# A routed eight-expert layer: tile experts read eight at a time, TensorE's first read put in front of tile 0, and one weighting moved on ScalarE

## The reference, cut to what matters

```
ys  = cond * 256**-0.5
d   = rsqrt((ys*ys) @ (W*W) + 1e-8)
y   = ((x * ys[:, None, :]) @ W) * d[:, None, :]
lang   = softmax(y @ lang_w.T + lang_b)                  # 4 languages
logits = y @ router_w.T + router_b + 0.1 * (lang padded, neighbours summed)
top_p, top_i = top_k(softmax(logits), 2);  top_p /= top_p.sum()
h   = gelu(y @ w1[e] + b1[e])                            # 256 -> 1024, exact gelu
out = h @ w2[e] + b2[e]                                  # 1024 -> 256
return x + sum over the two picked e of top_p * out
```

## Time and profile before

| | |
|---|---|
| median of 3 runs | 298.55 us (296.48 to 300.69) |
| profiled execution | 297.96 us, of which the span from first to last instruction is 296.2 us |
| TensorE busy (PE) | 272.3 us, 92% |
| ScalarE / VectorE / GpSimd busy | 195.7 / 189.2 / 179.4 us |
| mean granted TensorE clock | 0.976 |
| read from HBM, written | 27.61 MB, 9.64 MB |

### The profile page before, as it was taken

One profiled execution on the slowest core, in us unless ns is written; L12 is line 12 of the kernel. 1 busy time (PEld: TensorE's weight loads), 2 busy tenths in 40 slices (PEclk: granted clock), 3 DMA queues, 4 the chain that ended last, 5 costly groups with the idle time before them and its releaser, 6 DMA issues.

```text
span 296.2 us, 8964 instructions
## 1 busy us (share of the span) xinstructions
PE 272.3 (92%) x3066; PEld 223.1 (75%) x3066; DVE 189.2 (64%) x427; ACT 195.7 (66%) x426; POOL 179.4 (61%) x161
## 2 busy tenths in 40 slices
PE   8999988689999999999999999999999999999800
PEld 6878967588889998777777777777787878778400
DVE  1857788799699788565565565555655656556410
ACT  3356469599697898757767677677676676775500
POOL 8200056884666598676878577777767776464230
PEclk9999999979999999999999999999999999999975
DMA  6899996399874333465574644853544434323130
GB/s 145 325 400 388 353 348 206 109 314 460 306 191 90 56 57 72 56 101 65 76 91 77 87 70 78 76 91 64 83 77 74 75 74 76 51 39 38 20 35 0
DMA packets 39497, 39.93 MB, mean 135 GB/s; under 512 B 19504, under 2 KB 35328, under 8 KB 39296
## 3 DMA queue, kind: packets, MB, share of 16 engines
q1 hardware_dynamic: 31872, 28.89, 32.8%
q0 software_dynamic: 7552, 10.45, 23.0%
q10 hardware_dynamic: 32, 0.01, 0.0%
HBM read 27.61 MB, written 9.64 MB: 126 GB/s over the span
## 4 chain that ended last, share of the span: by engine, by line
PE 82%; DMA 5%; DVE 4%; issue 3%; ACT 2%; POOL 1%; POOLq 0%; DVEq 0%
PE ps L643 33%; PE ps L660 30%; PE ps L539 5%; PE ps L652 4%; PE ps L557 4%; DMA rows<-y_rows,idx 3%; DMA out<-onehot,idx 3%; PE ps L481 1%; PE ps L620 1%; DVE wsp L951 1%; PE ps L512 1%; PE ps L521 1%; ACT wsp L781 1%; PE ps L497 1%; POOL out L470 1%
## 5 line engine op out<-in xcount | busy, mean ns | idle before, releaser
L643 PEld LDWEIGHTS ps<-onehot,wsp 128*128 (+1 forms) x1872 | 130.7, 99 | 34.4 <-issue 1.1
L643 PE MATMUL ps<-onehot,wsp 128*128 128x128 f16 x1872 | 154.2, 220 | 0.8 <-ACT onehot L811 0.6
L827 ACT ACTIVATE pay<-ps,cur 128x128 f32<-128x128 f32 x312 | 117.4, 459 | 51.7 <-issue 37.9
L660 PE MATMUL ps<-wsp,pay 128*128 (+1 forms) x616 | 138.1, 316 | 1.2 <-DVE pay L1113 1.2
L470 POOL DMA_INDIRECT out<-onehot,idx x39 | 67.8, 1739 | 33.7 <-DMA out<-onehot,idx 15.3
L1113 DVE SCALAR_TENSOR_TENSOR pay<-pay,cur 128x512 f16<-128x512 f32 x72 | 54.9, 762 | 29.2 <-ACT pay L815 27.9
L439 POOL DMA_INDIRECT rows<-y_rows,idx x39 | 57.0, 1463 | 17.9 <-issue 11.0
L461 POOL TENSOR_SCALAR onehot<-onehot,cur 128x256 f32<-128x256 f32 x36 | 38.1, 1059 | 24.0 <-DVE onehot L1131 15.8
L660 PEld LDWEIGHTS ps<-wsp,pay 128*128 128x128 f16 x616 | 45.7, 97 | 6.9 <-issue 1.7
L1107 DVE TENSOR_SCALAR pay<-pay,cur 128x512 f16<-128x512 f32 x36 | 18.8, 521 | 26.0 <-ACT pay L827 26.0
L815 ACT ACTIVATE pay<-pay,cur 128x512 f16<-128x512 f32 x36 | 26.0, 722 | 1.2
(11 more groups left out here) (176 smaller groups left out, 195.5 us busy)
## 6 DMA issues: line engine op xcount, KB each, us to landing
stage<-in_L_ffn_w SPq DMA_DIRECT2D x9, 1024.0 KB, 10.6
wsp<-in_L_ffn_w SPq DMA_DIRECT2D x7, 1024.0 KB, 12.0
y_rows<-pay SPq DMA_DIRECT2D x4, 512.0 KB, 9.3
wsp<-in_x SPq DMA_DIRECT2D x3, 512.0 KB, 7.9
b2bc<-in_L_ffn_b SPq DMA_DIRECT2D x1, 1024.0 KB, 4.8
rows<-y_rows,idx POOLq DMA_INDIRECT x39
out<-onehot,idx POOLq DMA_INDIRECT x39, 4.1
wsp<-in_x SPq DMA_DIRECT2D x2, 256.0 KB, 5.5
```

The costliest lines, as they stand in the source:

```text
L643: last = mm(ps[:, HB + (2 * j + g) % RING, c * P:(c + 1) * P], wsp[:, bass.ds(e, 1), o:o + P].rearrange("p a f -> p (a f)"), xsp[:, j % RI ...
L660: last = mm(ps[:, OB + j % 2, 0:width], hsp[:, (2 * j + g) % NH, part, c, :], wsp[:, bass.ds(e, 1), o + w:o + w + width].rearrange("p a f ...
L827: last = a.activation(to, ps[:, HB + (2 * j + g) % RING, c * P:(c + 1) * P], ACT.Gelu, bias=cur[:, j % CURS, cc:cc + 1], scale=cur[:, j % ...
```

## The change

Three edits. BATCH goes from 31 to 8, so that each of the two engines reads `te` in four reads of 8, 8, 8 and 7 numbers (tiles 8, 16, 24, 32), each where the first tile of its batch is first asked for; on TensorE that is, from tile 16 on, in the middle of its list, behind the waits of the block with up(j, half 0) and in front of its first matmul. TensorE's first read, with its wait, moves from behind `sum_squares(3)` to in front of `transpose_rows(0)`. And on ScalarE `weigh(NT - 3)` moves from between the halves of the last tile to in front of `gelus(38, 0)`, behind `gelus(37, 1)`.

```diff
-BATCH = 31
+BATCH = 8
@@ TensorE
+            pe.wait_ge(te_ready, 1)
+            expert(E)
             transpose_rows(0)
             blocks((0, 0), None)
             transpose_rows(1)
             blocks((0, 1), None)
             sum_squares(3)
-            pe.wait_ge(te_ready, 1)
-            expert(E)
             for j in range(NT):
@@ ScalarE
             for j in range(NT):
-                if j == NT - 1:
-                    weigh(NT - 3)
                 gelus(j, 1)
                 if j + 2 < XACT:
                     copy_x(j + 2)
                 for n in HIGHS.get(2 * j + 1, ()):
                     split_high(n)
+                if j == NT - 2:
+                    weigh(NT - 3)
                 if j + 1 < NT:
                     gelus(j + 1, 0)
```

## The result

The changed kernel took 295.63 us in the median of 20 runs (294.85 to 298.01); the kernel before, beside it, 298.50 (296.07 to 300.69). The ratio is 0.9924 [0.9895, 0.9952], by which the change saves 2.3 us (2.9 by the medians). The profiled execution of after is one of its slowest, 298.01 us.

What follows compares the result with a forecast made beforehand. TensorE was taken to bound the kernel from about 60 to 272 us. On 297.96 us, -0.8 - 1.3 - 0.3 + 3.3 - 1.4 = -0.5 gave 297.5, set at 297.8 towards the median 298.55; range 294.8 to 301.5.

Steps and rivals of the forecast that it cites:

- First read moved, −0.8: At tile 2's transposes: TensorE's first read, moved before tile 0, costs nothing there and ends a wait, gaining 0.8 us.
- Clock behind it, −1.3: Behind tile 2's transposes, about 60 us: less idle time keeps TensorE's clock from falling, gaining 1.3 us.
- The first rival: At 60 us: the clock falls all the same, 1.3 us less gain, 298.8 us; chance 0.22.
- VectorE's shorter first read, −0.3: At tile 8, about 108 us: VectorE's read of 8 ends sooner, its part of h comes earlier, gaining 0.3 us.
- Three late reads, +3.3: TensorE at tiles 16, 24, 32: the array stands still 1.1 us at each read, costing 3.3 us (2.0 to 8.25).
- The size of a read: TensorE's read of 8 numbers: 0.55 us fixed plus 0.58 by the number, 1.15 us.
- The rival "all words": TensorE's late reads: time goes by the number alone, 0.72 us each, three stalls of 0.67, 296.2 us; chance 0.14.
- hardly 0.05 us of a read is covered: At TensorE's late reads: the sequencer is only 0.3 us ahead of the array, so queued matmuls hide almost nothing.
- The rival of hidden reads: TensorE's late reads: matmuls already queued cover them, three stalls of 0, 294.2 us; chance 0.06.
- The long read that takes the clock: TensorE's late reads: from about 1.7 us each, the idle time also halves the clock, 304.2 to 307.5 us; chance 0.08.
- VectorE's late reads, 0: VectorE's reads at tiles 16, 24, 32: hidden between parts of h in the wait for ScalarE, cost 0.
- The tail, −1.4: Last scatters: tile 36's no longer waits for ScalarE's weighting and follows the landing of the one before, gaining 1.4 us.

Runs made afterwards that it cites:

- the two comparisons: The changed kernel against the kernel before, measured twice with no edit between: 295.63 against 298.50 us, then 297.15 against 297.68 us.
- the pair with one read: Changed kernel with one TensorE read of 31 before tile 0, weighting at its old place or moved: 294.69 and 293.94 us, before 298.89.

## Why the prediction came out as it did

The forecast was 297.8 in a range of 294.8 to 301.5; measured were 295.63 and 297.15. The direction was right and small, as said, but the number owes something to luck: two terms of the sum had the wrong size, a cost 0.7 us too high and a gain 0.9 too low, and a third, a gain of 1.3, was not the change's own and nearly made up for both.

- *First read moved, −0.8*: −0.73 after, −0.75 where it alone was moved. Right, with its mechanism: the read of 2.80 us in front of tile 0 costs nothing either. Shown. The size holds where tile 2's rows land last. In four of the ten profiles with the new place (the second one of the changed kernel, both of the kernel with one read, and the one with other offsets) they had landed before, and to block (5, 0) it is 33.4 us, 1.4 less than the 34.74 of the old place without a fall.
- *Clock behind it, −1.3*: −1.6 between the two profiles, so the size of a fall was right (with the first term 2.3 together, against the 2.1 that I let pass VectorE). **The step from the read to the fall failed** (with the read gone the idle time shrinks, and the fall may go with it): the fall isn't bound to the read. The same idle time of 1.76 us in the same place had no fall behind it with only the weighting moved, nor had 1.77 us with VectorE's reads alone; filling it gave no time; and of the fourteen profiles six have a fall that begins at 48 to 52 us; in three of these the read stands at its old place, so behind the fall. What decides where it falls stays open. Moving the read does go with a higher mean clock: 0.980 or more in 21 of 66 executions with the read moved and in 1 of 100 with it at its old place. But this is no gain in time that can be seen: the three fastest executions of the changed kernel (294.85 to 295.06) had 0.973 to 0.978, the highest clocks (0.985 and 0.986) in the same comparison took 295.52 to 296.29, and the mean clock leaves out a part of the half-rate start. The difference of 2 us between the two comparisons is no larger than what the start alone does to an execution; how many runs of each had the late start was not recorded. The first rival, at 0.22 the second likeliest, had the price right (this term is none of the change's own gain), but not the place: none of the ten profiles with the read moved has a fall at 60 us.
- *VectorE's shorter first read, −0.3*: **this step failed.** Alone it gave −1.4. Two things in it were wrong. The first is the wait: I let VectorE's copy wait for GpSimd's weighting, until 111.31, and so gave VectorE 0.35 us; that wait did not exist, and VectorE gained 1.3. The second is what TensorE makes of it. I had measured that by how late the array was at 116.8, and there it is small in the trace of after as well (0.3 us, counted from block (7, 1)). But it was TensorE's *sequencer* that waited at the block's head for VectorE's part of h, 1.2 us later than need be. In before it came out of that with 0.2 us of lead; from then on it, not the array, set the pace, 2.71 us for a block on average up to block (15, 1), while the array needs 2.64 where its sequencer has lead: the gain on before grows from 0.28 us at block (9, 1) to 1.15 at block (15, 1), some 0.07 us a block. The 1.2 us come back as lead, which the array eats. The earlier trace rows showed this lead of 0.3 in the kernel before, and I used it for the reads' price only.
- *Three late reads, +3.3*: 2.5 measured, both as shift of the blocks and by taking them out. The size of a read was the step that failed: 1.15 us assumed for 8 numbers, the chip shows 0.60, outside the bounds of 0.8 to 1.6 that I had set for being right. The rival "all words" (0.72) was nearer, with 2.0 for the three; it missed that the read of 7 costs 1.07, and that the shift is a little more than the read's own length (0.70 for 0.60). The estimate from the Trainium skill, DMA: Bandwidth & Descriptors, section "Latency and other measured facts", 1.17, failed by more: its floor of about 600 ns is twice what a read of one number takes here (0.31); what it adds, that the compiler unrolls by four, fits the fours in these rows. The step "hardly 0.05 us of a read is covered" was right for the sequencer and wrong for the array: 0.26, 0.39 and 0.81 us of idle, since the lead that VectorE's edit had built (1.2 us) paid for the rest. The three stalls therefore don't show as 2.5 in the waits, and a reader of the waits alone would have said 1.5.
- *The rival of hidden reads* (a queue that holds work for the array) is refuted: each read delays the blocks by its whole length (0.63, 0.71 and 1.13 us for reads of 0.60, 0.60 and 1.07).
- *The long read that takes the clock*: refuted for these reads, as the longest idle was 0.81 us. Where reads are longer it comes true in part: 2.06 us of idle had no fall behind it, and 2.4 us had one that cost 1.8 us at once, near the 1.7 of the rival, and 1.0 by the end.
- *VectorE's late reads, 0*: no new wait of TensorE for VectorE in the middle tiles; right.
- *The tail, −1.4*: −1.46 between these profiles, 1.1 in the mean of all (4.1 us without the move, 3.0 with it). The mechanism is right, and the size is near the best case: the scatters land a little irregularly and then the move shows less (3.41 and 3.37 us instead of 2.85). By the medians of runs it could not be resolved (+0.13% by itself, 0.3 us in the pair with one read).

The account of the two profiles, at the last scatter: +2.47 from the start and −1.61 from the clock (neither the change's), −0.73, then from block (5, 0) to the last matmul −1.15 for the lead and +2.59 for the reads, and −1.46 in the tail: +0.11 (285.66 to 285.55). The change's own terms are −0.7 us in this pair; where tile 2's rows land early they are 0.7 better. The first comparison gave −2.3 by its ratio, the second −0.2, and 1.7 by the means of both. My sum had −1.3 for the clock, reads priced 0.7 us too high and VectorE's gain 0.9 too low; by itself each of these errors is larger than the −0.5 that came out. To this I had added half of the distance to the median.

The better kernel follows from the same terms: without its late reads on TensorE the change is worth −0.7 to −1.4, −1.1 and −1.1, so 2.9 to 3.6 us, and 1.6 more against an execution of before with the fall at 60 us. Its two sets of 6 runs gave 4.5 and 5.0 us by the medians, which is more than the terms give without that fall; runs of 6 leave about 1.3 us open either way.

## What to carry to other kernels

Where one engine sets the pace, look at two clocks of it, the array's and the sequencer's: a wait that cost the array 0.3 us here cost its sequencer 1.2, and in these blocks, whose matmuls carry registers, the lead was not rebuilt at the full clock (it stayed at 0.3 us). Put a read of registers where the engine waits anyway and read everything there; splitting a read pays only on the engine where the first number is what the others wait for. Batches of registers were cheapest here with a start and a length divisible by four. And before two profiles are compared, check whether both reached the first point behind the start at the same time; here executions of one program lay 2 to 3 us apart there.

## What the runs showed of the hardware

- A `TENSOR_LOAD` of int32 numbers from one partition into registers goes in fours where its start is divisible by 4: 1 number 0.31 us, 4 0.35, 8 0.60, 7 1.07, 31 2.80 on TensorE; from other starts each number costs about 0.26 to 0.33 (7 in 1.99, 10 in 2.62). On VectorE 8 take 0.60, 7 1.05, 31 3.06. An engine's first read is about 0.2 us longer (8 numbers 0.78 and 0.83). What in the program makes the fours was not looked into.
- TensorE's sequencer and array run nearly even on the blocks: 2.71 against 2.64 us for 32 matmuls with their register addresses; by an estimate from these, 1 us of the sequencer's lead lasts some 14 blocks.
- TensorE starts at half rate, until about 11 to 13 us in nine profiles and until 17 to 19 us in five, and this parts executions by 2 to 3 us at tile 0. The row of the granted clock can say 1.00 there: eight matmuls of L539 took 3.25 us in one such stretch and 2.04 at the full rate.
- The granted clock falls to 0.50 for some 3.4 us, but whether and where (near the start, at 48 to 52 us, at 60 us) differs between executions of the same work: idle times of 1.76, 1.77 and 2.06 us passed without one while 1.76 and 2.4 did not. One such stretch costs 1.6 us in the matmuls at 60 us, and in the blocks 1.8 us at once and 1.0 by the end, so single profiles can differ by as much as the change is worth.
